# Local attentions: values products directly ahead of the scores, with a new order of the stages on four engines

## The reference

```python
h = shift_token(x)
q, k, v = jnp.split(h @ wqkv, 3, axis=-1)       # 8 heads of 64
q, k = rotary_xpos(l2norm(q) * qs, l2norm(k) * ksc)
# windows of 64 rows; a window sees itself and the one before it
sim = jnp.einsum('bhwid,bhwjd->bhwij', bq * 8, bk)
attn = jax.nn.softmax(jnp.where(mask, -big, sim), axis=-1)
o = jnp.einsum('bhwij,bhwjd->bhwid', attn, bv)
x = x + o @ wo
```

## Time and profile before

| | us |
|---|---|
| three runs: median (lowest to highest) | 1139.02 (1138.47 to 1140.62) |
| profiled execution: span from the first to the last instruction | 1135.9 |
| profiled execution: its whole time | not listed |
| PE, DVE, ACT, POOL busy in the span | 1055.7, 889.0, 848.8, 674.1 |
| local attention 0: first scores to the start of its last output | 204.6 to 461.7 |
| local attention 1: the same | 542.0 to 798.4 |

### The profile page before, as it was taken

The page is one execution under the profiler, slowest core; times in us unless marked ns, Lnnn a source line. Parts: engine busy times, 40 slices in busy tenths (PEclk is TensorE's granted clock), DMA queues, the critical chain, the costliest instruction groups (busy, mean ns, idle before and its releaser), DMA issues. The chain is left out here.

```text
span 1135.9 us, 33920 instructions
## 1 busy us (share of the span) xinstructions
PE 1055.7 (93%) x11723; PEld 719.6 (63%) x11723; DVE 889.0 (78%) x2963; ACT 848.8 (75%) x2678; POOL 674.1 (59%) x1080
## 2 busy tenths in 40 slices
PE   6999998899999998898899999998998898999996
PEld 4667675577777776565577777776565588854442
DVE  4999996788888888564788888887685635289998
ACT  5788884799888898433798988987355866478886
POOL 4999995898888887201888888887233300011222
PEclk9999999999999999999999999999999999999999
DMA  7000000122222212321112121121001343000000
GB/s 242 7 2 12 12 3 1 38 48 58 58 48 57 48 40 47 112 59 35 37 36 60 37 48 44 45 48 41 20 1 40 94 127 84 20 10 16 17 18 18
DMA packets 66498, 50.86 MB, mean 45 GB/s; under 512 B 42262, under 2 KB 53442, under 8 KB 66050
## 3 DMA queue, kind: packets, MB, share of 16 engines
q1 hardware_dynamic: 66339, 48.84, 16.8%
HBM read 21.41 MB, written 2.38 MB: 21 GB/s over the span
## 5 line engine op out<-in xcount | busy, mean ns | idle before, releaser
L1259 PE MATMUL psum<-wa_wqkv,wa_hT 128*128 128x512 f32 x384 | 188.8, 600 | 2.5 <-DVE wa_tmp L1123 1.3
L1215 ACT ACTIVATE wa_p<-psum,wa_nb 128x128 f32<-128x128 f32 x512 | 183.8, 398 | 2.1 <-DVE wa_nb L1139 1.9
L1139 DVE CUSTOM_DVE_ANT_0 psum<-psum,wa_bias 128x128 f32<-128x128 f32 x512 | 133.0, 323 | 50.8 <-PE psum L1296 50.8
L1104 POOL TENSOR_TENSOR wa_p<-wa_p,wa_rrs 128x512 f32<-128x512 f32 x128 | 133.1, 1040 | 41.2 <-DVE wa_rrs L1148 41.2
L1812 POOL TENSOR_TENSOR ex_total<-ex_total,mod 128x128 f32<-128x128 f32 x32 | 15.5, 484 | 206.0 <-DVE ex_total L1940 206.0
L1075 POOL TENSOR_TENSOR wa_qr<-wa_qr,wa_tmp 128x512 f32<-128x512 f32 x64 | 81.6, 1275 | 76.4 <-DVE wa_tmp L1123 76.4
L1215 ACT ACTIVATION_READ_ACCUMULATOR wa_p<-psum,wa_nb 128x1 f32 x512 | 122.6, 239 | 0.0
L1987 ACT ACTIVATE cv_z_ex_yw<-psum,ex_w 128x128 f32<-128x128 f32 x384 | 106.7, 400 | 20.1 <-DVE ex_w L1916 7.4
L2058 PE MATMUL psum<-ex_wc,ex_hT 128*128 128x512 f32 x256 | 117.6, 602 | 3.4 <-DVE cv_z_ex_yw L1923 2.1
L1225 ACT ACTIVATE wa_pT<-psum 128x512 f32<-128x512 f32 x128 | 76.4, 597 | 38.6 <-PE psum L1273 38.6
L1123 DVE TENSOR_TENSOR wa_tmp<-psum,wa_tabs 128x512 f32<-128x512 f32 x128 | 87.2, 681 | 0.0
(11 more groups left out here) (264 smaller groups left out, 3001.5 us busy)
## 6 DMA issues: line engine op xcount, KB each, us to landing
wa_vm<-wa_v SPq DMA_DIRECT2D x127, 128.0 KB, 2.4
cv_toep<-cv_zpad SPq DMA_DIRECT2D x32, 136.0 KB, 2.6
cv_toep<-cv_zpad SPq DMA_DIRECT2D x16, 264.0 KB, 4.0
wa_tabs<-in_rotations_dram SPq DMA_DIRECT2D x2, 2048.0 KB, 7.8
wa_rows<-y_rows SPq DMA_DIRECT2D x31, 128.0 KB
wa_rows<-y_rows SPq DMA_DIRECT2D x31, 127.0 KB
x_rows<-in_L_attn_x_dram SPq DMA_DIRECT2D x4, 512.0 KB, 6.1
out_dram<-x_rows SPq DMA_DIRECT2D x32, 64.0 KB, 1.5
```

The source lines that it names most:

```text
L1104: nc.gpsimd.tensor_tensor(p, p, cols_bc(rrs[:, t % 2, r, :], P), ALU.mult)\
L1139: m = nc.vector.tensor_tensor_reduce(out=s, in0=s, in1=edges, scale=-1.0, scalar=MAX_FLOAT, op0=ALU.add, op1=ALU.min, accum_out=nb[:, t % ...
L1215: e = nc.scalar.activation(pr[:, t % 2, r, h, :], sim_bank[r][:, P * h:P * h + P], ACT.Exp, bias=nb[:, t % 2, r, h:h + 1], scale=-1.0, acc ...
L1259: nc.tensor.matmul(bank, hT[:, t % 3, :], wqkv[:, INNER * k:INNER * k + INNER], start=True, stop=True).then_inc(done.sem, 1)
```

## The change

Each of the four engines gets a new order of the stages of the local attentions. On PE the lags of `values` (4 to 5), `project_v` (2 to 3), `turn_k` (2 to 3) and `turn_p[0]` (3 to 4) go up by one, and `values` stands directly ahead of `scores`. On ACT `values` goes from lag 2 to 4, `k_columns` from 2 to 3 and `p_columns(0)` from 3 to 4. On POOL `add_q` goes ahead of `scale_p(0)`. On DVE the stages are in another order with the same lags. The squares and rotations now take k ahead of q, so the pairs of signals that share a semaphore are exchanged, and `norms` waits for the square of q. hT has four buffers in place of three, as v is projected a tile later. The filler products of `o_project` write bank 5 in place of bank 0. SP's program and the banks of the attentions stay as they are.

```diff
--- before.py
+++ after.py
@@ -788,7 +788,7 @@
 
         def o_project(t):
             if t >= TILES - 2:
-                idle_products(c, proj, TILES - t)
+                idle_products(c, bk[5], TILES - t)
             v_og.wait(pe, t)
             if t == TWO_BANKS:
                 v_og.wait(pe, TILES - 1)
@@ -982,7 +982,7 @@
     oT = ring("oT", 2, PAIRS, P)
     vs = ring("v", V_RING, INNER)
     kT = ring("kT", 3, PAIRS, P)
-    hT = ring("hT", 3, P)
+    hT = ring("hT", 4, P)
     sq = ring("sq", 2, 2, INNER)
     ss, ls, rn = ring("ss", 3, 2 * WH), ring("ls", 3, 2 * WH), ring("rn", 4, 2 * WH)
     qr, kr = ring("qr", 3, INNER), ring("kr", 3, INNER)
@@ -1001,8 +1001,8 @@
     p_h, a_h = signal("p_h"), signal("a_h")
     p_q, p_k, p_v = signal("p_q"), signal("p_k"), signal("p_v")
     a_v = signal("a_v")
-    a_sq, a_sk = in_turn("a_square_qk", 2)
-    v_q, v_k = in_turn("v_rotated_qk", 2)
+    a_sk, a_sq = in_turn("a_square_kq", 2)
+    v_k, v_q = in_turn("v_rotated_kq", 2)
     v_sum, g_ss = signal("v_sum"), signal("g_ss")
     g_k, g_q = signal("g_k"), signal("g_q")
     a_ls, a_rn = in_turn("a_log_inverse", 2)
@@ -1105,7 +1105,7 @@
                       .then_inc(g_p[r].sem, 1)
                 return f
 
-            return Phase([(scale_q, 2), (scale_k, 2), (scale_p(0), 3), (add_q, 1), (clip, 1),
+            return Phase([(scale_q, 2), (scale_k, 2), (add_q, 1), (scale_p(0), 3), (clip, 1),
                           (scale_p(1), 3), (add_k, 1)], first, TILES,
                          between=None if l else {s: lambda f=f: f(gp) for s, f in between.items()})
 
@@ -1125,7 +1125,7 @@
                 return f
 
             def norms(t):
-                a_sk.wait(dve, t)
+                a_sq.wait(dve, t)
                 g_ss.wait(dve, t - 3)
                 nc.vector.tensor_reduce(ss[:, t % 3, :], sq[:, t % 2, :, :].rearrange("p a (h d) -> p (a h) d", d=WD),
                                         AX_X, ALU.add).then_inc(v_sum.sem, 1)
@@ -1164,16 +1164,16 @@
 
             rotate_q = rotate(0, q_bank, a_sq, qr, p_tq, g_q, v_q)
             rotate_k = rotate(1, k_bank, a_sk, kr, p_tk, g_k, v_k)
-            return Phase([(row_max(0), 3), (o_columns, 5), (row_max(1), 3), (reciprocal(0), 3),
-                          (rotate_q, 1), (norms, 1), (reciprocal(1), 3), (rotate_k, 1), (residual, 5)], first, TILES,
+            return Phase([(o_columns, 5), (rotate_k, 1), (row_max(0), 3), (rotate_q, 1), (row_max(1), 3),
+                          (residual, 5), (norms, 1), (reciprocal(0), 3), (reciprocal(1), 3)], first, TILES,
                          between={1: tables_ready})
 
         def scalar(act):
 
             def h_columns(t):
                 p_h.wait(act, t)
-                p_v.wait(act, t - 3)
-                nc.scalar.activation(hT[:, t % 3, :], hw_bank[:, 0:P], ACT.Copy).then_inc(a_h.sem, 1)
+                p_v.wait(act, t - 4)
+                nc.scalar.activation(hT[:, t % 4, :], hw_bank[:, 0:P], ACT.Copy).then_inc(a_h.sem, 1)
 
             def square_q(t):
                 p_q.wait(act, t)
@@ -1226,9 +1226,9 @@
                       .then_inc(a_pT[r].sem, 1)
                 return f
 
-            return Phase([(inverse_norms, 2), (h_columns, 0), (p_columns(1), 4), (exps(0), 3),
-                          (square_q, 1), (square_k, 1), (q_columns, 2), (exps(1), 3), (k_columns, 2),
-                          (values, 2), (p_columns(0), 3)], first, TILES,
+            return Phase([(k_columns, 3), (square_k, 1), (inverse_norms, 2), (values, 4), (square_q, 1),
+                          (p_columns(0), 4), (h_columns, 0), (p_columns(1), 4), (exps(0), 3), (q_columns, 2),
+                          (exps(1), 3)], first, TILES,
                          begin=(lambda: nc.scalar.preload_act_table_set("natural_log_exp_and_others")) if l else None)
 
         def tensor(pe):
@@ -1256,7 +1256,7 @@
                     a_h.wait(pe, t)
                     first_use(name, t)
                     free.wait(pe, t - 1)
-                    nc.tensor.matmul(bank, hT[:, t % 3, :], wqkv[:, INNER * k:INNER * k + INNER], start=True,
+                    nc.tensor.matmul(bank, hT[:, t % 4, :], wqkv[:, INNER * k:INNER * k + INNER], start=True,
                                      stop=True).then_inc(done.sem, 1)
                 return f
 
@@ -1323,9 +1323,8 @@
             project_q = project(0, "q", q_bank, v_q, p_q)
             project_k = project(1, "k", k_bank, v_k, p_k)
             project_v = project(2, "v", v_bank, a_v, p_v)
-            return Phase([(scores, 3), (turn_h, 0), (turn_p[1], 4), (project_q, 1), (project_k, 1),
-                          (turn_q, 2), (output, 5), (project_v, 2), (turn_k, 2), (values, 4),
-                          (turn_p[0], 3)], first, TILES,
+            return Phase([(project_k, 1), (project_q, 1), (turn_k, 3), (values, 5), (scores, 3), (turn_p[0], 4),
+                          (turn_h, 0), (project_v, 3), (turn_p[1], 4), (output, 5), (turn_q, 2)], first, TILES,
                          begin=lambda: given.wait_layer(pe, l))
 
         readers = {"q": v_q, "k": v_k, "v": a_v, "hw": v_y, "turn": a_pT[1], "even": a_exp[0], "odd": a_exp[1], "o": v_oT}
```

## The result

The changed kernel takes 1150.24 us (median of four runs, 1148.73 to 1152.13), the kernel before 1139.82 (1138.47 to 1141.64) beside it: a ratio of 1.0098, 95% interval 1.0079 to 1.0118. It is slower by 10.4 us; the forecast was 1143.4, the range 1132 to 1151. The profiled spans differ by 11.0 (1135.9 in the earlier trace rows).

What follows compares the result with a forecast made beforehand. A loop over TensorE and ACT was taken to bound each step. -11.3 steady, -1.0 first steps, +5.9 and +2.2 waits, +5.2 layer ends, +3.4 half clock sum to +4.4 us on 1139.0: 1143.4, range 1132 to 1151.

Steps and rivals of the forecast that it cites:

- rival D: Values to scores on TensorE stays at 0.38: step 7.78, 5.9 us more, 1149.3; chance 0.57 together with the forecast.
- steady steps: Full steps of both local attention layers: 7.67 us in place of 7.88, 54 x 0.21 = 11.3 us gained.
- first steps: First steps of each layer, which are not full: 1.0 us gained, bounds -1 to +3.
- wait at tile 8: First layer: values wait 4.9 to 5.9 us for the copy of v, behind staging and MLP weights on SP; 5.9 taken.
- waits at tiles 12, 16, 20: First layer: paired stagings delay copies of v; 1.8 us at tile 12, 0.2 at the others, 2.2 taken.
- last scores to last output, both layers: Tile 31, each layer's end: 14.2 to 14.7 us in place of 11.6; 2.6 lost per layer, 5.2 in all.
- half clock: at tile 8; at the ends: TensorE's clock at 0.50 after waits: 1.7 us lost at tile 8, 1.7 at both layer ends (bounds 0 and 5.1).
- a loop through ACT: In each step a loop over TensorE and ACT takes 7.67 us, just above TensorE's own 7.62.
- Lead: ACT has copied v 5.3 us ahead of the values products that use it; SP's copy must fit in between.
- A: Late copies of v in the first layer never reach TensorE: -5.4 us, 1133.6; chance 0.16.
- C: The clock doesn't fall in the new gaps and waits take their lower bounds: -0.4 us, 1138.6; chance 0.17.
- B: Another loop, across four engines including DVE and POOL, needs 7.88 us or more a step: +15.7, 1154.7; chance 0.10.

Runs made afterwards that it cites:

- e4: Changed kernel with the transpose of h moved between values and scores on TensorE: 1160.81 us, ratio 1.0196 to the kernel before.
- e1: Changed kernel with ACT copying v two steps ahead of its use in place of one (values at lag 3): 1135.27 us, ratio 0.9972 to the kernel before.
- e2: Changed kernel with SP issuing the MLP weights ahead of the copies of tile 9, not tile 8: 1142.73 us, ratio 1.0044 to the kernel before.
- e8: e5 with the first portion of MLP rows staged ahead of tile 6, and two portions, not three, left for the layer's end: 1133.64 us, ratio 0.9955.
- e11: Changed kernel with the staging's copy of 127 partitions issued as two, of 112 and 15: 1136.06 us, ratio 0.9971 to the kernel before.
- e3: Changed kernel with TensorE running filler products during its waits for v at tile 8 and both layers' last tiles: 1142.43 us, ratio 1.0046.
- e5: e2 with SP's staging of MLP rows moved ahead of tiles 14, 18, 22, 26 and 30: 1139.3 us, ratio 0.9986 to the kernel before.
- e9: e8 with TensorE fillers at the layer ends and two ahead of the second layer's first transposes of q: 1133.43 us, ratio 0.9956.
- e12: e8 with the split of the 127-partition copy from e11: 1133.47 us, ratio 0.9950 to the kernel before.
- e10: e1 with the TensorE fillers of e9: 1135.08 us, ratio 0.9972 to the kernel before.
- e7: Changed kernel with GpSimd's earlier order, scale_p(0) ahead of add_q again: 1178.5 us, ratio 1.0348 to the kernel before.

## Why the prediction was right, and where a term was off

The direction, the mechanism and the places were right, and the size was 6.8 us short. The result lies 0.8 us inside the upper end of the range, which reached that far for rival D; D did not come, so that the range held is in part luck. The profiled difference of 11.0, one execution against one, by the prediction's own terms (intervals between scores, and from the last output to the next scores or the end):

| term | predicted | in the trace |
|---|---|---|
| steady steps | -11.3 (54 x 0.21) | -10.7 (53 x 0.202) |
| first steps | -1.0 | +1.1 |
| wait at tile 8 | +5.9 | +4.5 |
| waits at tiles 12, 16, 20 | +2.2 | +2.6 |
| last scores to last output, both layers | +5.2 | +5.6 |
| half clock: at tile 8; at the ends | +1.7; +1.7 | +1.6; +5.4 |
| the rest | | +0.9 |

- **The step**: 7.674 against 7.67 predicted, with values to scores at 0.21, where 0.22 was taken. The prediction named a loop through ACT as the bound, with TensorE at 7.62 just under it. The trace and e4 put it the other way: TensorE's order, plus 0.05 for the copy of p(1) ahead of the transposes of q. When e1 makes that copy 0.05 later, the step grows by 0.05. At such a distance the two could not be told apart on paper.
- **Lead and queue**: lead 5.4 (5.3 predicted), tile 8 waits 4.5, just under the lower of the two ends (4.9 and 5.9). The slow issue of 1.52 in the earlier trace rows, which I took as a fixed price, was an accident of that execution: it is 0.54 now. That the queue is the cause is shown by e2, e8 and e11, which leave all four engines alone.
- **The layer ends**: the length was right, the reason only in part. The copy is worth 1.6 of 2.7 (e1); I laid all of it to the copy and missed that the exponentials of the last tile start 1.2 later in the new order.
- **The clock at the layer ends** is the term that failed: "I count half, 1.7 in all". It cost 2.7 behind the first layer (the 68.9 and 66.2 at e3; the kernel before has 66.2 too), 1.4 behind the second (70.35 and 68.95; the kernel before has 68.95 too), and 1.3 at a fall at 445.5, ahead of the first layer's end, that I had not counted (the last two intervals between scores take 17.1, in the second layer 15.8). With the third, its bound of 5.1 was too low as well. e3 shows the first two. The third has no experiment: the fall at about 440 to 445 came in e3, e5 and e9 too and not in e1, e2 or e12. Nor is it shown what makes the clock fall at the start of the second layer: it does so twice in the trace of the kernel before (one is the earlier trace rows), once in that of the change, and not in those of e1, e9, e10 and e12. The Trainium skill (TensorE: Matmul & The Clock Gate, HAM oscillation), taken for all three waits, said 1.7 more than the sum; the trace agrees with it at all three.
- **The first steps** gained nothing: the first eight intervals take 64.5 us, 64.6 before, with 9.29, 7.99 and 8.18 among them where the sum had most of them at 7.67. No run looked into that.
- **The rivals**: A and C are out in the change itself; e1 is what A described (11 us of lead), at 1135 where A was priced at 1134. B didn't come, but e7 shows it real with one stage moved back. D fell: 0.21 and not 0.38.

## What to carry to other kernels

When lags change, subtract producer from consumer again for every transfer between them, and compare the new lead with the worst gap in the queue that issues it; here an in-order queue with a gap of 15 us from copy to copy did no harm until the lead was 5. Before reordering around a slow issue, ask why it is slow: here splitting one DMA of 127 partitions into 112 and 15 took a staging from 8.0 to 3.2 us. A wait of a few microseconds on TensorE is to be priced with the half clock that followed it here: 1.4 to 2.7 us for waits of 2.4 to 4.5.

## What the runs showed of the hardware that was not expected

- SP's issue of 1 KB took 6.5 us behind a copy of 127 partitions and 0.77 behind one of 112 and one of 15. The slow row of a queue need not be the slow DMA.
- The price of a change of TensorE's shape depends on what stands around it: 0.10 between four transposes and values, 0.15 between one transpose and scores (e4).
- The time of one and the same kernel goes with its mean granted clock. Of the 20 runs of the kernel before beside e11, the five at 0.986 took 1141.65 to 1142.34 us and the two at 0.995 1135.16 and 1135.52: 6.8 us apart in the mean. A difference of two or three us between kernels needs many runs for that reason, and one profiled execution doesn't show it.
